# Attention scores of two heads side by side on half the rows of TensorE each, with two-head score groups, eight probability buffers and low parts moved to GpSimd

## The reference, cut to what matters

```python
# x: 8 sequences of 1024 tokens, 256 wide; 16 heads of 64, latent rank 128
latent_kv = x @ w_kv_down
k, v = split(latent_kv @ w_kv_up)
q = x @ w_q
att = einsum('bqhd,bkhd->bhqk', q, k) * HEAD_SIZE ** -0.5
att = softmax(where(causal, att, -inf))
y = einsum('bhqk,bkhd->bqhd', att, v) @ w_out
x = layernorm(x + y)
# then 8 experts (hidden 1024, gelu), each on the 257 tokens of a sequence that score highest,
# added up, and a second layernorm of the sum with x
```

## Time and profile before

| what | value |
|---|---|
| median of 3 runs | 3080.33 us (3075.99 to 3082.09) |
| profiled execution | 3079.45 us, span 3077.6 us |
| TensorE matmuls busy | 2989.0 us (97%) |
| VectorE, ScalarE, GpSimd busy | 2078.5, 1910.1, 1539.3 us |
| DMA traffic | 542.01 MB, mean 176 GB/s |

### The profile page before, as it was taken

The page is one execution under the profiler, slowest core; times in us unless marked ns, Lnnn a source line. Parts: engine busy times, 40 slices in busy tenths (PEclk is TensorE's granted clock), DMA queues, the critical chain, the costliest instruction groups (busy, mean ns, idle before and its releaser), DMA issues. The chain is left out here.

```text
span 3077.6 us, 62761 instructions
## 1 busy us (share of the span) xinstructions
PE 2989.0 (97%) x19264; PEld 2393.8 (78%) x19264; DVE 2078.5 (68%) x5938; ACT 1910.1 (62%) x4173; POOL 1539.3 (50%) x1623
## 2 busy tenths in 40 slices
PE   8999999999999999999999999999989999999996
PEld 6776767777776776776767677689989999999996
DVE  6777777777777777777767767745968865545446
ACT  6676777777677767676767767645534444444443
POOL 4444444444444444444444434446757776666665
PEclk9999999999999999999999999999989999999998
DMA  7776877787777777777778687677634444434425
GB/s 183 202 205 184 205 207 192 200 212 186 204 207 191 196 204 196 194 201 212 185 203 210 188 204 200 166 245 268 237 122 118 107 102 107 106 79 90 112 50 164
DMA packets 394705, 542.01 MB, mean 176 GB/s; under 512 B 78696, under 2 KB 293480, under 8 KB 394368
## 3 DMA queue, kind: packets, MB, share of 16 engines
q1 hardware_dynamic: 352320, 487.43, 58.0%
q0 software_dynamic: 25152, 33.75, 6.6%
q10 hardware_dynamic: 16896, 16.78, 1.5%
HBM read 211.85 MB, written 158.16 MB: 120 GB/s over the span
## 5 line engine op out<-in xcount | busy, mean ns | idle before, releaser
L288 POOL TENSOR_SCALAR prob<-prob,inv 128x128 f32<-128x128 f32 (+7 forms) x1024 | 766.6, 752 | 1130.3 <-DVE inv L760 1129.9
L755 DVE CUSTOM_DVE_ANT_0 s_ps<-s_ps,mask 128x128 f32<-128x128 f32 (+7 forms) x1024 | 774.0, 756 | 444.3 <-PE s_ps L455 438.1
L644 ACT ACTIVATE prob<-s_ps,neg_max 128x128 f32<-128x128 f32 (+7 forms) x1024 | 760.2, 743 | 214.5 <-DVE neg_max L755 206.2
L470 PE MATMUL t_ps<-ident,prob 128*128 128x128 f32 x3328 | 525.6, 274 | 20.1 <-POOL prob L288 13.7
L470 PEld LDWEIGHTS t_ps<-ident,prob 128*128 128x128 f32 x3328 | 393.4, 140 | 69.8 <-POOL prob L288 17.5
L737 ACT ACTIVATE prob_t<-t_ps 128x512 f32<-128x512 f32 x512 | 305.8, 597 | 207.4 <-PE t_ps L470 207.1
L1821 PE MATMUL e_y<-w_hi,hid_hi 128*128 128x256 f32 (+1 forms) x1088 | 312.0, 287 | 0.0
L1822 PE MATMUL e_y<-w_lo,hid_hi 128*128 128x256 f32 (+1 forms) x1088 | 308.0, 283 | 0.0
L1823 PE MATMUL e_y<-w_hi,hid_lo 128*128 128x256 f32 (+1 forms) x1088 | 308.0, 283 | 0.0
L1682 POOL DMA_INDIRECT acc_d<-yg,idx_all x128 | 211.3, 1651 | 189.9 <-ACT yg L1895 161.1
L454 PE MATMUL s_ps<-w_lo,w_hi 128*128 128x512 f32 (+3 forms) x768 | 291.6, 382 | 7.4 <-ACT prob L644 7.4
(11 more groups left out here) (264 smaller groups left out, 6736.3 us busy)
## 6 DMA issues: line engine op xcount, KB each, us to landing
k_hh<-k_high SPq DMA_DIRECT2D x128, 256.0 KB, 4.5
y_d<-c_res SPq DMA_DIRECT2D x128, 256.0 KB, 4.3
k_lz<-k_low SPq DMA_DIRECT2D x126, 256.0 KB, 5.4
s_d<-squares SPq DMA_DIRECT2D x63, 512.0 KB, 2.9
late_t<-s_d SPq DMA_DIRECT2D x252, 128.0 KB, 3.4
w_lo<-k_high SPq DMA_DIRECT2D x124, 256.0 KB, 4.5
c_yt<-y_d SPq DMA_DIRECT2D x60, 512.0 KB, 7.0
s_d<-squares SPq DMA_DIRECT2D x63, 384.0 KB, 2.6
```

The lines of the kernel that those rows point to most:

```text
L288: pool.tensor_scalar(pr, pr, inv[:, s % 4:s % 4 + 1], 1.0, ALU.mult, ALU.mult).then_inc(norm_done, 1)
L470: mm = pe.transpose(t_ps[s % 2][:, to * P:(to + 1) * P], prob[s % 4][:, j * P:(j + 1) * P], ident[:])
L644: act.activation(prob[s % 4][:, 0:(q + 1) * P], score_part(s), ACT.Exp, scale=-1.0, bias=neg_max[:, s % 4:s % 4 + 1], accum_out=total[:, s ...
L755: dve.tensor_tensor_reduce(part, part, mask[:, T - (q + 1) * P:T], 1.0, -MASKED, ALU.add, ALU.min, neg_max[:, s % 4:s % 4 + 1]).then_inc(m ...
```

## The change

- **Scores.** `scores(n, u, q)` issues both heads of query tile q at once. For each chunk of up to 512 columns it runs three products (high x high, high x low, low x high), each as two matmuls: head 0 on partitions 0 to 63 into `s_ps[0]`, head 1 on partitions 64 to 127 into `s_ps[1]`. Queries and keys are read from the projections' high and low tensors as they are, which are double-buffered over pairs; the stacks, the ten placing DMAs a pair and their waits are gone.
- **Waits and slots.** Tile q's scores are issued in slots 0, 1, 5, 7, 9, 11 for q = 2 to 7, and in slots 13 and 14 for tiles 0 and 1 of the next pair. For q from 4 on they wait for both exps of tile q - 1 (`exp_done >= 16n + 2q`), for q = 2 and 3 for both of tile q - 2, and for the next pair's for all exps of this pair. Maxima are issued two at a time, exps one ahead of and one behind the slot's copy.
- **Buffers.** Eight buffers of probabilities, row sums and maxima instead of four.
- **Reciprocals.** In the four narrow tiles one `reciprocal` serves both heads (`invert_both`).
- **Low parts** of x and latents are subtracted on GpSimd.

```diff
+    PB = 8
...
-        SCORES_AT = [[4], [5], [6], [7], []] + [[s + 3] for s in range(5, 13)] + [[16], [17, 18], [19]]
...
+        SCORES_AT = {0: 2, 1: 3, 5: 4, 7: 5, 9: 6, 11: 7, 13: 8, 14: 9}
+
+        EARLY_INVERSES_AT = {6: [8, 9], 8: [10], 10: [12], 12: [14]}
+        PAIRS_INVERTED_AT = {2: 4, 3: 6, 14: 16, 15: 18}
+        MAXIMA_AT = {0: [4, 5], 1: [6, 7], 5: [8, 9], 7: [10, 11], 9: [12, 13], 11: [14, 15], 13: [16, 17], 14: [18, 19]}
+        INVERSES_AT = {8: [11], 10: [13], 12: [15]}
+
+        EXPS_AT = {1: [5], 2: [7], 6: [9], 8: [11], 10: [13], 12: [15], 14: [17], 15: [19]}
+        LATE_EXPS_AT = {0: [4], 1: [6], 5: [8], 7: [10], 9: [12], 11: [14], 13: [16], 14: [18]}
...
+            def x_split(b, i):
+                k, cols = x_piece(b, i)
+                pool.wait_ge(x_high, 4 * b + i + 1)
+                pool.sem_inc(passed, 1)
+                pool.tensor_tensor(xt_lo[:, k, cols], xt[:, k, cols], xt_hi[:, k, cols].bitcast(F32), ALU.subtract
+                                   ).then_inc(x_low, 1)
...
-            def place_queries(n, u):
-
-                sp.wait_ge(low_done, 4 * n + 2)
-                sp.sem_inc(passed, 1)
-                queries(u, slice(0, T))
...
-            def scores(n, u, s):
-                g, q, h = step(s)
+            def scores(n, u, q):
                 cols = slice(q * P, (q + 1) * P)
-                width = (q + 1) * P
-                for c in range(g + 1):
-                    w = slice(c * HALF, min((c + 1) * HALF, width))
-                    out = score_part(s)[:, w]
-
-                    pe.matmul(out, q_hl[u][h][:, cols], k_hh[u][h][:, w], start=True, stop=False)
-                    mm = pe.matmul(out, q_hl[u][h][:, cols], k_lz[u][h][:, w], start=False, stop=True)
-                mm.then_inc(scores_done, 1)
+                for c in range(q // 4 + 1):
+                    w = slice(c * HALF, min((c + 1) * HALF, (q + 1) * P))
+                    for i, (a, b) in enumerate(((q_high, k_high), (q_high, k_low), (q_low, k_high))):
+                        for h in range(2):
+                            rows = slice(64 * h, 64 * h + 64)
+                            mm = pe.matmul(score_part(2 * q + h)[:, w], a[u][rows, cols], b[u][rows, w],
+                                           start=(i == 0), stop=(i == 2))
+                            if c == q // 4 and i == 2:
+                                mm.then_inc(scores_done, 1)
...
+                    q = SCORES_AT.get(s, 0)
+                    if 2 <= q < 8:
+                        pe.wait_ge(exp_done, 16 * n + (2 * q - 2 if q < 4 else 2 * q))
+                        scores(n, u, q)
+                    elif q and after:
+                        pe.wait_ge(low_done, 4 * n + 8)
+                        pe.wait_ge(exp_done, 16 * n + 16)
+                        scores(n + 1, 1 - u, q - 8)
...
+            def invert_both(n, s):
+                i = s % PB
+                dve.wait_ge(exp_done, 16 * n + s + 2)
+                dve.reciprocal(inv[:, i:i + 2], total[:, i:i + 2]).then_inc(inv_done, 2)
```

More of the change, by code:

```diff
@@ L305, in slots @@
                         norm(n, s + 2)
+                    if (m, s) in X_SPLIT and not last_batch(n):
+                        x_split((n >> 3) + 1, X_SPLIT.index((m, s)))
+                    if latents(n, m, s - 1) is not None:
+                        l_split((n >> 3) + 1, latents(n, m, s - 1))
                     if s == W_SPLIT and after >= 2:
@@ L328, in store_y @@
                              y[g][:]).then_inc(y_out[g], 16)
[L330 to L342, removed]
             def write_squares(n, w):
@@ L606, in slots @@
                 for s in range(8 * g, 8 * g + 8):
-                    for t in SCORES_AT[s]:
-                        if t < 16:
-                            if first and t == 8:
-                                keys_ready(0)
-                            pe.wait_ge(exp_done, 16 * n + (t - 3 if t < 8 else t - 1))
-                            scores(n, u, t)
-                        elif after:
-                            if t == 16:
-                                keys_ready(n + 1)
-                            pe.wait_ge(exp_done, 16 * n + (15 if t % 2 == 0 else 16))
-                            scores(n + 1, 1 - u, t - 16)
+                    q = SCORES_AT.get(s, 0)
[6 more added lines that the diff above has]
+                        scores(n + 1, 1 - u, q - 8)
                     turn(n, s)
@@ L708, in first @@
                 high(1, 1, 0)
-                exp(0, 0)
-                exp(0, 1)
+                for s in range(4):
+                    exp(0, s)
             def slots(n, m, g, after):
@@ L739, in slots @@
                     for t in LATE_EXPS_AT.get(s, []):
-                        exp(n, t)
+                        if t < 16 or after:
+                            exp(n, t)
                     if s - 1 in Q_AT and after >= 2:
@@ L838, in slots @@
                     for t in EARLY_INVERSES_AT.get(s, []):
-                        invert(n, t)
-                    for t in MAXIMA_AT[s]:
+                        if t < 16 or after:
+                            invert(n, t)
+                    if s in PAIRS_INVERTED_AT and (s < 8 or after):
+                        invert_both(n, PAIRS_INVERTED_AT[s])
+                    for t in MAXIMA_AT.get(s, []):
                         if t < 16 or after:
                             maximum(n, t)
-                    for t in INVERSES_AT[s]:
+                    for t in INVERSES_AT.get(s, []):
                         if t < 16 or after:
@@ L854, in slots @@
                         copy_late(n, s)
-                    for t in LATE_MAXIMA_AT.get(s, []):
-                        if after:
-                            maximum(n, t)
-                    if (m, s) in X_SPLIT and not last_batch(n):
-                        x_split((n >> 3) + 1, X_SPLIT.index((m, s)))
-                    if latents(n, m, s - 1) is not None:
-                        l_split((n >> 3) + 1, latents(n, m, s - 1))
                     if s - 1 in Q_AT and after >= 2:
```

127 lines of the change are left out of this document (44 added, 83 removed).

## The result

The changed kernel takes 3315.62 us (median of 4 runs, 3314.09 to 3317.64) beside 3079.01 us for the kernel before on the same chip: ratio 1.077, interval 1.075 to 1.079. The prediction was 3327 us, range 3231 to 3427. The profiled execution has a span of 3315.0 us, against 3077.6.

The account below looks back on a forecast made before the run. TensorE's own work was taken to bound attention. A pair changes by -2.2 + 2.6 + 4.7 - 1.0 = +4.1 us; 63 pairs give 258, less 10 for latents: 3079 + 248 = 3327 us, range 3231 to 3427.

Parts of the forecast that it names:

- Part 3: Scores of a query tile wait for both exps of the tile before: three TensorE gaps, 4.7 us a pair lost.
- Parts 1 and 2: Score matmuls in attention: half-height form gains 2.2 us a pair, changes of the array's shape cost 2.6.
- 1.0 us of bare loads: Exposed weight loads in the old score groups, counted again in the shape-change entries: 1.0 us a pair taken off.
- part 1: Score chunks: three half-height steps for two heads instead of four full-height matmuls, full overlap, 2.2 us a pair gained.
- Latent projection: In seven pairs the next batch's latent projection, 1.4 us, falls into the last gap: 10 us back.
- parts 5 and 6: Low parts moved to GpSimd, and one reciprocal for two heads in narrow tiles: off the path, 0.
- Part 4: Ten placing DMAs a pair and their SyncE queue waits go: 0, perhaps up to 3 us at kernel start.
- A: Score groups: the array does not drain for a row shape when the next load is ready; 3231 us, chance 0.11.
- B: Score steps: the two heads' loads go one after the other, +100 us, 3427 us; chance 0.11.
- C: Score matmuls: the two halves do not overlap at all, +418 us, 3745 us; chance 0.06.
- D: Part 3's gaps do not open; parts 1 and 2 remain, 3041 us, with A about 2945; chance 0.05.
- E: Attention: the new gaps lower TensorE's granted clock; given nearly nothing.

Follow-up runs that it names:

- experiment 1: The changed kernel with the same operations in another order on each engine, nothing left out; 3085.12 us, ratio 1.0014 to the kernel before.
- experiment 7: The changed kernel with the value products of head group 0 in slot 12 instead of 13; 3275.43 us, ratio 1.064.
- experiment 3: The changed kernel with both heads' half-height score matmuls on the same 64 rows, head 0 computed twice; 3799.96 us, ratio 1.234.
- experiment 4: The changed kernel with score loops exchanged: head 0's three products first, then head 1's, instead of alternating; 3320.55 us, ratio 1.078.
- experiment 2: The changed kernel in its own order, but with two full-height score matmuls per head; 3283.32 us, ratio 1.066.
- experiment 6: The changed kernel plus eight unused 256 KB transfers a pair on SyncE's queue; 3390.65 us, ratio 1.102.
- experiment 5: The changed kernel with low parts subtracted on VectorE again and separate reciprocals for each narrow step; 3318.44 us, ratio 1.078.
- experiment 8: Experiment 1's kernel with latent projection halves a turn earlier, GpSimd's x subtractions and ScalarE's latents copy moved; 3071.33 us, ratio 0.9976.

## Why the prediction was right, point by point

From the ninth exp of the first pair to the ninth of the last, the kernel before takes 1957.9 us and the changed one 2186.1 us, 228.2 more; 10 more lie at the two ends of attention, and the stages behind it are 0.8 us shorter. Pair periods through the second sequence, us:

```
before  31.44  30.33  30.25  30.21  31.90  31.18  33.84  30.25
after   34.13  34.15  34.13  34.12  34.12  34.13  38.10  34.17
```

- **The steady pair.** 34.3 us predicted, 34.13 measured: 63 x 3.89 = +245 us, against 63 x 4.1 = 258.
- **Part 3, the waits: right in place and size.** The three gaps were put at 1.30, 1.81 and 1.61 and came as 1.22, 1.66 and 1.62, 4.50 a pair instead of 4.7; tile 6 has none, as said. The chain for 1024 columns was put at 4.10 and is 4.22 (0.36 + 1.15 + 1.36 + 1.20, and 0.15 instead of 0.05 to hand over), and the work within it at 2.49 and is 2.60; the two misses cancel in the gap. Experiments 1 and 7 show that the gaps are a matter of the order: filled, they go.
- **Parts 1 and 2, the form: right in sum.** Busy time falls by 0.51 us a pair where -2.2 + 2.6 - 1.0 = -0.6 was counted. Full overlap holds (experiments 3 and 4). The array's drain holds as well: the four last matmuls of tile 7 start within 1054.46 to 1054.69, the last streams 0.21 us, and the next load starts at 1055.01, 0.1 us later. It is 0.09 to 0.11 us in 380 of the 381 changes from scores of 256 to 512 columns to transposes, and 0.15 in nearly all of the 127 from scores of 128 columns. What the sum had wrong is what it is compared with. The 1.0 us of bare loads taken off were credited to the half-height form, but experiment 2 shows that full-height matmuls in the new grouping shed 0.29 of the 0.51 as well (30.13 to 29.84), so that the form itself gains 0.22 of busy time. And part 1's gain was counted in full where the chain sets the pace: there first results come no earlier than at full height, so the saved matmul time turns into longer waits (0.58 us a pair), while the narrow groups pay their changes of shape in full. In this order the form alone is a loss of 0.36 us a pair (experiment 2).
- **Latent projection: wrong sign.** It was to fill the last gap and give 10 us back. The query projection behind it now waits for the latents' copy (14 times, 16.6 us), and the odd pair costs 3.95 us over its neighbours against 3.60 before: 7 x 0.35 = +2 us. The step counted the matmuls and not who reads them next. (This is the second half of the odd pair; its first half is under parts 5 and 6.)
- **Part 4, the placing transfers: mis-sized.** Taken as 0, with a row that speaks of TensorE only the earlier trace rows. In the list above two pairs of the kernel before, 31.44 and 31.90, are 1.2 and 1.7 us over 30.25; both hold waits of VectorE for its written squares. Over all of attention the kernel before has 27 us beyond steady pairs and latents, the changed kernel 8. Some 21 of the 27 lie in 13 pair periods that hold such waits (some 3 of them are lost to a low clock, in two of these periods); the changed kernel has no such wait, and its 8 lie in pairs with a low clock. So some 13 us came back here; the other 6 are under parts 5 and 6. That the placing transfers caused the waits is argued: experiment 6 shows that transfers in this queue can bring them about, with others, at another place.
- **Parts 5 and 6** (low parts, reciprocals): put at 0, and experiment 5 finds no difference (2.8 us, the two intervals overlap). But the kernel before did pay at this place, which the prediction did not see: the period of 31.18 us, 0.93 over a steady one, comes back in seven sequences, 6.5 us in all, and the changed kernel has nothing there (34.13). It is the first half of pair 6, where x is split; VectorE's low part stands ahead of a maximum, and TensorE stands 0.78 us for the exp behind it:

```profile
463.11 0.69 DVE L802 TENSOR_TENSOR b_xt_lo<-b_xt,b_xt_hi 128x512 fp32r<-128x512 f32 x1 [0.35 <-ACT b_xt_hi L676]
463.72 0.82 DVE L755 CUSTOM_DVE_ANT_0 s_ps<-s_ps,mask 128x640 f32<-128x640 f32 x1
...
464.63 0.79 ACT L644 ACTIVATE prob<-s_ps,neg_max 128x640 f32<-128x640 f32 x1 [0.77 <-DVE neg_max L755]
465.57 0.50 PE L454 MATMUL s_ps<-w_lo,w_hi 128*128 128x512 f32 x1 [0.78 <-ACT prob L644]
```

  Since experiment 5 has the low parts back on VectorE without this loss, the new slots alone remove it; what the move to GpSimd would give the kernel before was not tried.
- **Sum.** +245 + 2 - 19 = +228 in the middle, +10 at the ends (2.6 ahead of that first exp, 7.4 behind the last), which were not costed. Against the forecast these are -13, +12, -19 and +10: the total misses by only 11 us (+237 against +248) because misses of both signs cancel. That the gaps are the loss is no luck; that the total is this close is in part.

Rivals: A (no drain) is excluded by the drain in the rows, B (loads in turn) by loads of the two heads 3 ns apart and steps of 0.12 us at 256 columns and 0.23 us at 512, C by experiment 3. D's premise failed, since all three gaps opened; its figure without gaps, about 3041 us, is approached by experiment 8 (3071), whose 30.05 us a pair are 0.4 over that rival's 29.6, with six changes of shape fewer. E has a little truth: 20 us at the low clock against 7, some 7 us, where next to nothing was given.

## What to carry to other kernels

When two units of work are joined into one instruction group, list who waits for the last of them and count, in the new order, how much other work the bound engine has until then: here 4.5 us a pair of missing cover outweighed everything done to the matmuls, and most of it came back with another order. Price a form in the order in which it will run: where a chain sets the pace, only an earlier first result is worth anything, and engine time saved there becomes waiting. And ask of every transfer that is removed or added what stands behind it in its queue, and who waits for that, before it is put at zero.

## What the runs showed of the hardware that was not expected

- Matmuls on rows 0 to 63 and 64 to 127 overlap fully, twelve in six spacings (with both heads on the same rows TensorE is busy 6.6 us more a pair), and also when three of one half are issued before the first of the other (1.65 against 1.66 us).
- TensorE's granted clock fell to 0.50 after idle times of 1.66 and 1.63 us in the pair shown, for 3.4 us, yet the changed kernel has these idle times in every pair and fell in 5 places of attention only (four of them looked at, each within 2 us of such an idle time; the kernel before fell after idle times of 2.22 and 2.19 us), while experiment 3, with more streaming and shorter waits, fell in 57. What sets it off stays open.
- A change from 64-row scores to 128-row transposes cost 0.09 to 0.11 us between the end of the last stream and the next load (0.15 behind scores of 128 columns), at 505 of 508 changes.
- Eight transfers of 256 KB a pair, put into SyncE's queue, held one 256 KB write back by 3.8 us and took its landing from 2.0 to 4.4 us, with the DMA engines busy for 0.57 of their time instead of 0.32; that stalled VectorE in 57 places and TensorE in 36.
